# An attention block and a gated feed-forward network on one core: gate and up of three chunks by seven block products, with the weight block sums made beside the decoding

## The reference, cut to what matters

```python
# attention over 8 batches of x[256, 512]: 16 heads of 16 channels, masked softmax over 512 keys
Q, K, V = (proj(Wq), proj(Wk), proj(Wv))
att = softmax(mask(einsum('bhqd,bhkd->bhqk', Q, K) / sqrt(Dh)))
y = einsum('bhqk,bhkd->bhqd', att, V)                 # -> xt, [8 * 256 rows, 512]
# feed-forward; each weight is a 4-bit code times a scale per 32 inputs
Wg, Wu, Wd = (dequant_nvfp4(packed, scales) ...)      # [4096, 512], [4096, 512], [512, 4096]
gate = einsum('th,nh->tn', xt, Wg)
up = einsum('th,nh->tn', xt, Wu)
inter = gelu_tanh(gate) * up
out = x + einsum('tn,hn->th', inter, Wd)
```

## Time and profile before

| | |
|---|---|
| two timed runs | 1427.59 and 1433.02 us, median 1430.3 |
| the profiled execution | 1430.62 us |
| its span, first to last instruction | 1428.7 us |
| mean granted clock of TensorE | 0.987 |
| busy: PE, DVE, ACT, POOL | 1381.1, 840.9, 750.7, 467.7 us |

### The profile page before, as it was taken

One profiled execution on the slowest core, in us unless ns is written; L12 is line 12 of the kernel. 1 busy time (PEld: TensorE's weight loads), 2 busy tenths in 40 slices (PEclk: granted clock), 3 DMA queues, 4 the chain that ended last, 5 costly groups with the idle time before them and its releaser, 6 DMA issues.

```text
span 1428.7 us, 19828 instructions
## 1 busy us (share of the span) xinstructions
PE 1381.1 (97%) x7632; PEld 556.7 (39%) x7632; DVE 840.9 (59%) x993; ACT 750.7 (53%) x856; POOL 467.7 (33%) x374
## 2 busy tenths in 40 slices
PE   4798899999999999999999999999999999999999
PEld 1222233334334344444334444444444444444444
DVE  6787876677776676666666666666765421111111
ACT  1466686677766666665555666555556621111111
POOL 3011143345533343343333344334334421111110
PEclk8898999999999999999999999999999999999999
DMA  4312344533544315422143125232012224332220
GB/s 122 113 62 61 125 132 122 161 122 131 163 148 139 131 67 172 127 90 89 67 127 86 79 89 184 90 127 87 29 64 89 89 89 149 139 125 89 89 89 30
DMA packets 50702, 152.99 MB, mean 107 GB/s; under 512 B 7328, under 2 KB 20768, under 8 KB 50608
## 3 DMA queue, kind: packets, MB, share of 16 engines
q1 hardware_dynamic: 48869, 150.52, 30.7%
q10 hardware_dynamic: 1739, 1.20, 0.4%
HBM read 113.66 MB, written 37.77 MB: 106 GB/s over the span
## 4 chain that ended last, share of the span: by engine, by line
PE 92%; DVE 4%; ACT 1%; issue 1%; DMA 1%; POOL 0%; ACTq 0%; DVEq 0%
PE psum L1025 16%; PE psum L1027 15%; PE psum L1026 15%; PE psum L1073 8%; PE psum L1075 8%; PE psum L1074 8%; PE psum L961 5%; PE psum L927 4%; PE psum L995 4%; PE psum L977 3%; PE psum L905 3%; DVE maxima L771 2%; PE psum L915 1%; PE psum L1002 1%; DVE maxima L778 1%
## 5 line engine op out<-in xcount | busy, mean ns | idle before, releaser
L1025 PE MATMUL psum<-y_hi,w_ring 128*128 128x512 f16 x1024 | 389.7, 381 | 0.0
L1026 PE MATMUL psum<-y_lo,w_ring 128*128 128x512 f16 x1024 | 388.2, 379 | 0.0
L1027 PE MATMUL psum<-y_hi,w_ring 128*128 128x512 f16 x1024 | 388.2, 379 | 0.0
L778 DVE TENSOR_REDUCE maxima<-psum 128x2 f32<-128x1024 f32 x192 | 233.5, 1221 | 74.9 <-PE psum L927 73.2
L575 POOL CAST big<-big 128x1024 f16<-128x1024 f32 x128 | 145.0, 1133 | 386.2 <-ACT big L707 386.0
L588 POOL TENSOR_TENSOR in_lo<-inter,in_hi 128x512 f16<-128x512 f32 x128 | 152.7, 1193 | 350.5 <-ACT in_hi L686 350.4
L707 ACT ACTIVATE big<-psum 128x1024 f32<-128x1024 f32 x128 | 131.0, 1023 | 175.7 <-PE psum L961 175.0
L818 DVE SCALAR_TENSOR_TENSOR inter<-psum,gelu 128x512 f32<-128x512 f32 x128 | 88.2, 689 | 222.9 <-PE psum L1027 205.9
L828 DVE SCALAR_TENSOR_TENSOR acc<-psum,acc 128x512 f32<-128x512 f32 x128 | 88.3, 691 | 198.7 <-PE psum L1075 197.8
L1073 PE MATMUL psum<-w_ring,in_hi 128*128 128x512 f16 x512 | 194.6, 380 | 0.0
L1075 PE MATMUL psum<-w_ring,in_lo 128*128 128x512 f16 x512 | 194.1, 379 | 0.0
(11 more groups left out here) (80 smaller groups left out, 1275.8 us busy)
## 6 DMA issues: line engine op xcount, KB each, us to landing
w_ring<-w_parts SPq DMA_DIRECT2D x96, 768.0 KB, 7.2
w_parts<-w_ring SPq DMA_DIRECT2D x32, 768.0 KB, 4.2
dq_scales<-scales SPq DMA_DIRECT2D x32, 384.0 KB
qk_parts<-wide SPq DMA_DIRECT2D x62, 128.0 KB
wide<-qk_parts SPq DMA_DIRECT2D x62, 128.0 KB
small<-x SPq DMA_DIRECT2D x8, 512.0 KB, 4.5
acc<-x SPq DMA_DIRECT2D x4, 1024.0 KB, 6.2
out<-acc SPq DMA_DIRECT2D x16, 256.0 KB, 5.8
```

Of the source, the lines that this page charges most:

```text
L778: nc.vector.reduce_max(maxima[:, g % 2, n // 2:n // 2 + 9:8], psum[:, bank:bank + 2, :], AX.X).then_inc(max_red, 2)
L1025: nc.tensor.matmul(dst, w[:, 0, k % 2, cols], hi, start=(k == 0), stop=False)
L1026: nc.tensor.matmul(dst, w[:, 0, k % 2, cols], lo, start=False, stop=False)
L1027: return nc.tensor.matmul(dst, w[:, 1, k % 2, cols], hi, start=False, stop=(k == TT - 1))
```

## The change

Chunk 0 is computed as before. In chunks 1 to 3 two neighbouring units make a pair, and gate and up of a pair are each a 2 by 2 block product: weights by halves of the inner dimension and by unit, y by halves of the inner dimension and by batch. Such a product is made from seven block products instead of eight, by sums of blocks (Winograd's form of Strassen's scheme). A block product here is for one of gate and up (`m`): two inner blocks by three matmuls of 256 columns. The two banks 2 and 3 take turns (`part_bank`); a bank holds gate and up of one product.

- Products 0, 3 and 4 are copied out by ACT into `pair_c` (`keep_part`), products 1, 2, 5 and 6 are added by DVE (`sum_part`), and POOL makes three further sums in SBUF (`mix_part`). Then ACT takes one gelu of 1024 elements, DVE one product (`pair_inter_part`), ACT two roundings (`pair_high`), POOL two low parts (`pair_low`). `pair_c` exists once.
- The down product of a pair is half of a group of four units: two output row blocks ("pieces"), each 12 matmuls of 512 columns, in the same two banks. The sum of matmuls of the down product is unchanged.
- The sums of y are made by POOL when a quad of an odd batch is finished (`split_sums`, ten instructions where there were two).
- The sums of the weights are made in shared stage 0: per pair POOL makes four more sums (`weight_sums`), ACT and DVE split them (`sums_hi`, `sums_lo`), SP writes them out. A pair is read back by one DMA of 1792 KB (`load_fast`) and one of 512 KB (`load_down`).
- `p_exp` has three slots instead of four, so in the opening `A0` stands before `S30`; buffers share memory in other ways, and the decoded weights `dq_w` have two slots.

```diff
+A11, A12, A22, S3, S4, S1, S2 = range(BLOCKS)
+B11, B21, B22, T1, T2, T3, T4 = range(BLOCKS)
+PRODUCTS = ((A11, B11), (S2, T2), (A12, B21), (S1, T1), (S3, T3), (S4, B22), (A22, T4))
+        def fast_chunk(c):
+            for r in range(PAIRS * (c - 1), PAIRS * c):
+                late = [("fast", r - 1, None, name, None) for name in ("gelu", "inter", "halves")] if r == 2 else []
+                for n in range(len(PRODUCTS)):
+                    for m in range(2):
+                        yield late + [("fast", r, None, "product", (n, m))]
+                        late = []
+                steps = [(g, half, n, i) for g, half in pieces_after(r) for n in range(2) for i in range(GROUP)]
+                for at, (g, half, n, i) in enumerate(steps):
+                    late = [("fast", r, None, {2: "gelu", 4: "inter", 6: "halves"}[at], None)] if at in (2, 4, 6) else []
+                    yield [("fast", r, None, "down", (g, half, n, i, at // GROUP))] + late
...
+        def weight_sums(pool, p):
+            even, odd = dq_w[:, 0], dq_w[:, 1]
+            pool.wait_ge(w_f_s, 2 * p + 2)
+            wait_from(pool, s_lo_s, 2 * p)
+            wait_apart(pool, pool_spare, w_lo_s, W_HALVES * (2 * p + 1))
+            nc.gpsimd.tensor_tensor(even[:, 0], even[:, 0], odd[:, 0], ALU.subtract).then_inc(s_f_s, 1)
+            wait_apart(pool, pool_spare, s_f_s, 4 * p + 1)
+            nc.gpsimd.tensor_tensor(s_sums[:, 1], odd[:, 1], even[:, 0], ALU.subtract).then_inc(s_f_s, 1)
...
+            def mix_part(r, n):
+                if n == 3:
+                    pool.wait_ge(part_sum, 4 * r + 1)
+                    wait_apart(pool, pool_spare, part_kept, 3 * r + 2)
+                    nc.gpsimd.tensor_tensor(pair_c[:, :, C12], pair_c[:, :, C12], u2, ALU.add).then_inc(part_mix, 1)
+                    return
...
+                pool.wait_ge(part_mix, 3 * r + 1)
+                wait_apart(pool, pool_spare, part_kept, 3 * r + 3)
+                nc.gpsimd.tensor_tensor(pair_c[:, :, C22], pair_c[:, :, C12], pair_c[:, :, C21], ALU.add).then_inc(part_mix, 1)
+                wait_apart(pool, pool_spare, part_mix, 3 * r + 2)
+                nc.gpsimd.tensor_tensor(pair_c[:, :, C21], pair_c[:, :, C21], u2, ALU.add).then_inc(part_mix, 1)
...
+            def keep_part(r, n):
+                act.wait_ge(part_mm, len(PRODUCTS) * r + n + 1)
...
+                    act.wait_ge(pair_inter, r)
+                    act.wait_ge(pair_lo, 2 * r - 1 if n == 0 else 2 * r)
+                nc.scalar.copy(pair_c[:, :, {0: C11, 3: C12, 4: C21}[n]],
+                               part_bank(len(PRODUCTS) * r + n).rearrange("p (m t) -> p m t", m=2)).then_inc(part_kept, 1)
...
+            def part_free(r, n):
+                if r == 0 and n < 2:
+                    pe.wait_ge((gelu_s, inter_s)[n], UNITS)
+                elif r == 2 and n < 2:
+                    pe.wait_ge(part_sum, 4 * r - 1 + n)
+                elif n < 2:
+                    pe.wait_ge(piece_add, pieces_to(r - 1) - 1 + n)
+                elif n in (3, 4):
+                    pe.wait_ge(part_sum, 4 * r + {3: 1, 4: 2}[n])
+                else:
+                    pe.wait_ge(part_kept, 3 * r + {2: 1, 5: 2, 6: 3}[n])
...
+                dst = part_bank(len(PRODUCTS) * r + n)[:, C * m:C * m + C]
+                for k in range(2):
+                    w = [fast_w[:, r % 2, block, a, (2 * k + m) * P:(2 * k + m + 1) * P] for a in range(2)]
+                    y = [ffn_y[:, (c + 1) % 2, a, moving, k, :] for a in range(2)]
+                    nc.tensor.matmul(dst, w[0], y[0], start=(k == 0), stop=False)
+                    nc.tensor.matmul(dst, w[0], y[1], start=False, stop=False)
+                    last = nc.tensor.matmul(dst, w[1], y[0], start=False, stop=(k == 1))
```

More of the change, by code:

```diff
@@ L259, in plan @@
                     continue
[L260 removed]
+                if step[0] in "dhl" and (step[1] == "0") != first or step[0] == "c" and first:
                     continue
@@ L696, in _ @@
                         gelu_part(u)
+                    elif step == "U0" and u % 2 and u < UNITS - 1:
+                        sums_hi(act, (u + 1) // 2, 0)
+                    elif step == "G2" and u and u % 2 == 0 and u < UNITS - 1:
+                        sums_hi(act, u // 2, 1)
+                    continue
+                if kind == "fast":
+                    if step == "halves":
+                        pair_high(b)
+                    elif step == "gelu":
+                        pair_gelu_part(b)
+                    elif step == "product":
+                        n, m = arg
+                        if (b, n, m) == (0, 0, 0):
+                            inter_high(UNITS - 1)
+                        if m and n in (0, 3, 4):
+                            keep_part(b, n)
                     continue
@@ L728, in _ @@
                     weight_hi(act, int(step[1]))
+                elif step in ("c1", "c3") and b < SOLO:
+                    sums_hi(act, 0, int(step[1]) // 2)
         @block.vector
@@ L882, in _ @@
                     weight_lo(dve, int(step[1]))
+                elif step in ("c2", "c4") and b < SOLO:
+                    sums_lo(dve, 0, int(step[1]) // 2 - 1)
         @block.tensor
```

540 lines of the change are left out of this document (403 added, 137 removed), and 16 rows, old and new, of the table PLAN.

## The result

The changed kernel takes **1563.6 us** (median of two runs, 1563.49 to 1563.64) where the kernel before takes 1430.3. The recorded ratio is 1.092, with a 95% interval of 1.0896 to 1.0944 (the two medians give 1.093). The forecast was 1424, with a range up to 1456, so it was wrong, by 140 us and in its sign. The profiled execution has a span of 1561.6 us and a mean granted clock of 0.954, against 1428.7 us and 0.987.

The account below looks back on a forecast made before the run. PE was taken as the bound, busy 97% of the span, so fewer or shorter matmuls help behind the opening. 1430.6 - 57 + 5 + 3 + 28 + 9 + 6 = 1424.6, so 1424 us, range 1386 to 1456.

Parts of the forecast that it names:

- Products, -57: Gate and up of 48 pairs: 84 matmuls of 256 columns at 0.109 us replace 48 at 0.2158, 57 us off.
- Rival 3: Matmuls of 256 columns miss their rate, 0.025 us more for each of 4032, total 1525 us; chance 0.02.
- The reloads: Reading back a pair's weights takes 5.8 us, hidden and costing nothing while a pair takes over 8 us.
- Last stage, +8: PE 0.3 us late per pair before the next first piece, +5; the last pair's low parts at the end, +3.
- Stage 0 and opening, +6: Making the weight sums delays the decoding by 0.25 us a pair, +4, and the opening by +2; bounds -2 and +28.
- 2.6 us of cover in each bank: In stage 0, PE's other work in each bank was to hide weight_hi coming some 2 us later.
- rival 2: VectorE's queue becomes the bound; stage 0 loses 1.6 us a pair, stages 1 and 2 2.1; 1487 us, chance 0.12.
- Stages 1 and 2, +28: PE waits for VectorE's sums and adds, 1.0 us for 26 pairs and 0.3 for six; bounds 0 and 67.
- quads and borders, +9: POOL's longer y split makes PE 2 us late at three chunk borders, 6, and delays mixes, +3; bounds 0 and 20.
- the 0.7 us for it: In stages 1 and 2, time added per pair for four p_low slowed beside POOL's extra operations.
- a trifle of 3 us: Within chunks, the split on POOL delays the mixes once or twice for each odd batch, +3 us.
- The granted clock: Remark that the opening's clock was 0.95 at such a PE load, which would add to rival 2; no size given.

Follow-up runs that it names:

- e9: Changed kernel without weight block sums, with the old wait of one decoded unit at a time, POOL's split shortened and mixes on 16 of 256 columns: 1421.4 us.
- the doses: Two runs of the kernel before with extra scratch operations per pair: four on POOL, 1451.5 us; two on ACT and two on VectorE, 1476.5 us.
- e8: Changed kernel with POOL's three mixes of a pair cut to 16 of 256 columns, all waits kept: 1533.4 us.
- e7: Changed kernel with POOL's split of an odd batch's quad cut from ten instructions to four, leaving out the six sums of y: 1530.5 us.
- e4: Changed kernel where POOL's scale multiplication for an odd unit no longer waits for VectorE's splitting of the pair before: 1564.2 us.

## Why the prediction was wrong

- **Products, -57: right.** 0.109 us for 256 columns, and with little waiting left (e9) PE's busy time is down by 47 us. Rival 3 fell. The 81 ns that the Trainium skill's page "TensorE: Matmul & The Clock Gate", Back-to-back issue gap, gives for 128 columns isn't met by the earlier trace rows, and the row of 256 columns follows. The reloads are hidden, as said: no wait of PE is put down to them.
- **Last stage, +8: right in the mechanism.** The wait ahead of the first piece, for VectorE's add behind POOL's mix, is there, 6.2 us in 15 pairs against 5, and at the end one of 2.3 us for POOL's low part against 3. All idle time rose by 10.5, and busy time by 6.3 over what I had, of which 1.6 is the lower clock. The stage gave 2.3 us instead of 11.
- **Stage 0 and opening, +6: the step that failed.** It measured 97. I took 0.25 us for a pair, with "2.6 us of cover in each bank". I had named the right chain (`sums_lo`, `weight_f`, `weight_hi`, the gelu), and about the right load (VectorE from 70 to 86%; it stood at 80 and 84 of 100 us from 205 to 305 and from 305 to 405 us, 77% over the stage). What I left out is what the trace had already shown for `p_low`: that VectorE is blocked beside POOL. I charged the new work of a pair (4 x 1.19 on POOL, 2 x 1.02 on ACT, 2.4 or more on VectorE: 9 us or more for each 20 us) at the engines' free durations and gave it to engines that looked free at 70%. I also took it that `weight_f` would be 2 us later, where behind a quad's split ACT waited for it for 6.5 us and PE's cover gave way by up to 8.3. The sums cost 70 us here, 60 by the doses, which hold nothing else of the changed kernel. The upper bound of +28 is rival 2's 1.6 us for each of 16 pairs and 2, and the 1.6 has no working. Of the rest, e9 shows that the split explains 12.7 (345.6 to 332.9; the mixes have no place in stage 0, as e8 shows), and 6 stay open: the halved high and low parts and the ring of three slots were not tried apart.
- **Stages 1 and 2, +28, and quads and borders, +9: too small, and one reason wrong.** Together 76 us, 57 of idle time and 19 of busy time, 15.5 of it by the lower clock. VectorE's load didn't reach the 85 to 90 of 100 us; it was 258.1 of 357.0, 72%, and `p_low` kept its 1.48 us, so the 0.7 us for it was wrong. What I had as a trifle of 3 us is the split: e7 gives 26 us for it in these stages. e8 gives 21 for the mixes, which I had only through `p_low` and in the last stage. The three border waits were 4.0 us against 6.
- **The granted clock: not in the sum.** It stood in rival 2 as a remark. It took 36 us of PE's busy time, a fifth of the 190 us that were lost. In stage 0 its mean fell to 0.93 (part of the time at 1.2 instead of 2.4 GHz) with PE idle for 16% of the time; in the last stage, with PE idle for 5%, it was 0.99. Whether a full clock would have given all of it back isn't shown: in e4 stage 0 ran at 0.95 and was as long, with more idle time.
- **Rival 2** had the place and the mechanism, the gelu late behind `weight_hi`. Its price of 1.6 us for a pair was measured as (65.2 + 24.1) / 16 = 5.6 us, so its 1487 was 77 us short as well.
- **The range** has ends, 1386 and 1456, that aren't those its sentence names (1395 and 1459). It makes no difference to the outcome.
